# Mixed weight products between the halves of the neighbour products, y_hi ahead of relu on ScalarE, and the last neighbour products in other PSUM banks

## What is computed

```python
idx = top_k(-(sq[:, :, None] + sq[:, None, :] - 2 * einsum('bdn,bdm->bnm', xyz, xyz)), 8)   # xyz = ctx_4096, (4, 1601, 512)
for i in range(4):                                   # twice over: 8 layers in all
    shortcut = points                                # (4, 256, 512)
    p = where(points >= 0, points, 0.01 * points)
    g = neighbours of every point by idx             # (4, 256, 8, 512)
    c = einsum('oi,bin->bon', w[i], p)
    gn = einsum('oi,bikn->bokn', w[i], g)
    points = (c + gn.sum(axis=2)) / 9 + shortcut
```

## Time and profile before

| what | us |
|---|---|
| median of 3 runs | 337.64 (336.52 to 339.07) |
| the profiled execution | 334.24 |
| its span, first to last instruction | 332.5 |
| PE busy | 320.8 |
| DVE busy | 258.5 |
| ACT busy | 174.0 |
| POOL busy | 95.0 |

### The profile page before, as it was taken

The page is one execution under the profiler, slowest core; times in us unless marked ns, Lnnn a source line. Parts: engine busy times, 40 slices in busy tenths (PEclk is TensorE's granted clock), DMA queues, the critical chain, the costliest instruction groups (busy, mean ns, idle before and its releaser), DMA issues.

```text
span 332.5 us, 5114 instructions
## 1 busy us (share of the span) xinstructions
PE 320.8 (97%) x2024; PEld 290.9 (88%) x2024; DVE 258.5 (78%) x333; ACT 174.0 (52%) x255; POOL 95.0 (29%) x85
## 2 busy tenths in 40 slices
PE   4999999999999899999899999999999999999995
PEld 4999999999899788888788889888888888889884
DVE  3994799799699676888867796887869867796773
ACT  4584397485564726454836644626455264644510
POOL 2011111111133214333644441426335063441400
PEclk9999999999999999999999999999999999999999
DMA  7979859969700000000000000000000000000023
GB/s 236 353 209 264 223 146 239 279 150 251 188 0 1 2 0 2 0 0 2 1 2 0 1 3 0 0 2 0 2 0 0 2 0 2 0 0 2 38 92 126
DMA packets 8608, 23.41 MB, mean 70 GB/s; under 512 B 772, under 2 KB 2052, under 8 KB 8584
## 3 DMA queue, kind: packets, MB, share of 16 engines
q1 hardware_dynamic: 7288, 18.36, 16.3%
q0 software_dynamic: 1296, 4.72, 8.3%
HBM read 20.98 MB, written 2.10 MB: 69 GB/s over the span
## 4 chain that ended last, share of the span: by engine, by line
PE 41%; DVE 8%; ACT 2%; issue 1%; DVEq 0%
PE wide L423 24%; PE wide L412 6%; PE wide L401 5%; PE wide L399 5%; DVE y_rest L722 2%; DVE y_lo L726 2%; DVE r_mixed L662 2%; DVE state L734 2%; ACT y_hi L570 2%; ACT relu L562 1%; PE wide L385 0%; ACT r_high L565 0%; DVEq L709 0%; DVEq L725 0%
## 5 line engine op out<-in xcount | busy, mean ns | idle before, releaser
L279 POOL TENSOR_TENSOR r_low<-relu,r_high 128x512 fp32r<-128x512 f32 x64 | 84.8, 1339 | 140.4 <-ACT r_high L565 140.4
L423 PE MATMUL wide<-adj,y_hi 128*128 128x512 f32 (+1 forms) x260 | 102.3, 394 | 0.8 <-DVE state L734 0.8
L423 PE MATMUL wide<-adj,y_lo 128*128 128x512 f32 (+1 forms) x260 | 101.7, 393 | 0.0
L722 DVE TENSOR_TENSOR y_rest<-wide,y_hi 128x1024 f32<-128x1024 f32 x32 | 39.2, 1224 | 45.4 <-ACT y_hi L570 45.4
L562 ACT ACTIVATE relu<-state 128x512 f32<-128x512 f32 x64 | 40.2, 628 | 46.5 <-DVE state L734 33.7
L399 PE MATMUL wide<-w_high,r_high 128*128 128x256 f32 x256 | 62.2, 281 | 0.9 <-DVE y_rest L722 0.9
L401 PE MATMUL wide<-w_low,r_low 128*128 128x256 f32 x256 | 61.9, 280 | 0.0
L570 ACT CAST y_hi<-wide 128x1024 fp32r<-128x1024 f32 x32 | 32.3, 1008 | 54.8 <-PE wide L401 54.8
L423 PEld LDWEIGHTS wide<-adj,y_hi 128*128 128x128 f32 x260 | 48.9, 188 | 11.7 <-DVE state L734 1.2
L423 PEld LDWEIGHTS wide<-adj,y_lo 128*128 128x128 f32 x260 | 49.0, 188 | 10.5 <-issue 0.2
L399 PEld LDWEIGHTS wide<-w_high,r_high 128*128 128x128 f32 x256 | 48.3, 189 | 2.3 <-issue 1.1
(11 more groups left out here) (57 smaller groups left out, 290.6 us busy)
## 6 DMA issues: line engine op xcount, KB each, us to landing
raw<-in_ctx_dram SPq DMA_DIRECT2D x23, 512.0 KB, 5.4
g_low<-in_ctx_dram POOLq DMA_DIRECT2D x9, 512.0 KB, 6.2
state<-in_x_dram SPq DMA_DIRECT2D x4, 512.0 KB, 7.1
out_dram<-state SPq DMA_DIRECT2D x3, 512.0 KB, 2.8
w_raw<-in_fside_BxSxS_dram SPq DMA_DIRECT2D x1, 1024.0 KB, 11.2
rest_raw<-in_ctx_dram SPq DMA_DIRECT2D x4, 130.0 KB
raw<-in_ctx_dram SPq DMA_DIRECT2D x2, 256.0 KB, 3.3
out_dram<-state SPq DMA_DIRECT2D x1, 256.0 KB, 2.0
```

The costliest lines, as they stand in the source:

```text
L279: nc.gpsimd.tensor_tensor(r_low[:, n % 3, h, :], relu[:, h, :], r_high[:, n % 3, h, :].bitcast(fp32), ALU.subtract).then_inc(r_low_ready, 1)
L423: mm = nc.tensor.matmul(bank[to][:, cols], part[:, s % 2, q, h * P:(h + 1) * P], adj[:, b, q, cols], start=(q == 0 and part is y_hi), stop ...
L722: nc.vector.tensor_tensor(y_rest[:, :, :], wide[MAIN][:, :].rearrange("p (q o) -> p q o", q=NB), y_hi[:, s % 2, :, :].bitcast(fp32), ALU.s ...
```

## The change

Five edits:

- PE: the mixed products become a function of their own, `y_mixed`, and are issued between the two halves of the neighbour products of the step before (in step 0 right behind the main products).
- ACT: `y_high(s)` comes ahead of `relu_parts(s+1)`.
- DVE: `split_y` is cut in two. The order is y_rest of s, update of s-1 half 0, y_lo of s, (in step 1 distances and relu_mixed(2)), update of s-1 half 1, relu_mixed(s+1).
- The last neighbour products go to banks 6, 7 and 0.
- They wait for the updates of step 29 in place of those of step 30.

```diff
-        LAST_OUT = ((0, ALL, 4), (1, slice(0, N // 2), 5), (1, slice(N // 2, N), 0))
+        LAST_OUT = ((0, ALL, 6), (1, slice(0, N // 2), 7), (1, slice(N // 2, N), 0))
...
-            def y_step(s, w):
+            def y_main(s, w):
...
                 mm.then_inc(main_done, 1)
+
+            def y_mixed(s, w):
+
                 if s == 0:
                     pe.wait_ge(gram_ready, (B - 1) * NB + 3)
                 pe.wait_ge(r_mixed_ready, s + 1)
...
-                for n, (h, cols, to) in enumerate(pieces):
+                for n, (h, cols, to) in pieces:
...
-                y_step(s, l % BLOCKS)
+                y_main(s, l % BLOCKS)
+                if s == 0:
+                    y_mixed(s, l % BLOCKS)
...
-                    out_step(s - 1, STEPS[s - 1][1], out_pieces(s - 1))
+                    first_half, second_half = out_pieces(s - 1)
+                    out_step(s - 1, STEPS[s - 1][1], [first_half])
+                    y_mixed(s, l % BLOCKS)
+                    out_step(s - 1, STEPS[s - 1][1], [second_half])
...
-            pe.wait_ge(state_ready, CH * LAST_STEP)
-            out_step(LAST_STEP, STEPS[LAST_STEP][1], LAST_OUT)
+            pe.wait_ge(state_ready, CH * (LAST_STEP - 1))
+            out_step(LAST_STEP, STEPS[LAST_STEP][1], out_pieces(LAST_STEP))
...
             for s in range(B * LAYERS):
+                y_high(s)
                 if s + 1 >= B - 1 and s + 1 <= LAST_STEP:
                     relu_parts(s + 1)
-                y_high(s)
...
-            def split_y(s):
+            def y_remainder(s):
...
+            def y_low(s):
+
                 dve.wait_ge(mixed_done, s + 1)
...
-                split_y(s)
+                y_remainder(s)
+                if s > 0:
+                    update(s - 1, 0, ALL, 2 * out_at(s - 1), 0)
+                y_low(s)
                 if s == 1:
                     distances(B - 1)
                     relu_mixed(2)
                 if s > 0:
-                    update(s - 1, 0, ALL, 2 * out_at(s - 1), 0)
+                    update(s - 1, 1, ALL, 2 * out_at(s - 1) + 1, 1)
                 if B - 1 <= s + 1 <= LAST_STEP:
                     relu_mixed(s + 1)
-                if s > 0:
-                    update(s - 1, 1, ALL, 2 * out_at(s - 1) + 1, 1)
```

More of the change, by code:

```diff
@@ L146, in out_at @@
             return FIRST_WIDE if s < ENTER or s % 2 == 0 else SECOND_WIDE
+        assert out_at(LAST_STEP) == SECOND_WIDE
         def by_dma(b, k):
@@ L428, in out_pieces @@
             def out_pieces(s):
-                return LAST_OUT if s == LAST_STEP else tuple((h, ALL, 2 * out_at(s) + h) for h in range(CH))
+                return enumerate(LAST_OUT if s == LAST_STEP else ((h, ALL, 2 * out_at(s) + h) for h in range(CH)))
             for b in range(B):
```

## The result

The changed kernel takes 344.49 us (median of 4 runs, 344.02 to 345.14); the kernel before, 337.6 (4 runs). The ratio is 1.0213, with a 95% interval from 1.0176 to 1.0251: slower, by 6.9 us. The interval is clear of no change; whether the loss is more or less than 2% it does not tell.

What follows compares the result with a forecast made beforehand. PE was taken as the bound late (6.60 us of work a step), an ACT-DVE ring early (7.15). A new 7.13 us ring gave +9.8, the end -1.04, so +8.7 on 337.64: 346.3 us, range 341 to 353.

Steps and rivals of the forecast that it cites:

- y_hi ahead of relu: ACT's new order: the deciding term, making a loop of 7.13 us a step against 6.60 of PE's work.
- the ring: Loop over ACT, POOL and PE: main products, y_hi, relu and r_high twice, r_low twice, next main products; 7.13 us.
- 27c-183.8: Change of total time in us, where c is the length of one turn of the ring, forecast at 7.13.
- DVE's new order: DVE's reordered work: room enough, no cost after step 2; the early loop through ACT and DVE opens.
- r_low and r_mixed never meet: POOL and DVE: the new order keeps these two apart, so the pair of r_low stays at 2.55 us.
- Mixed products between the halves: PE: waits for r_mixed go, at most 0.07 us per late step, 0.55 per early; later y_lo, cover 2.3, costs nothing.
- Step 2: Mixed products now behind the wait for the state update: main(3) starts at 128.1 instead of 127.16, a lasting loss.
- Other banks: Last neighbour products: their wait for the update of the step before goes, -1.04 us (0 to -1.1).
- Rival 1: Faster, 332.0 us: r_low chain hidden, early ring opens, PE's 6.60 sets each step; needs c below 6.81; chance 0.05.
- Rival 2: About even, 337.2 us: POOL's r_low ready some 0.34 earlier than recorded, ring 6.79; chance 0.06.
- Rival 3: Slower still: PE learns of POOL's end 0.5 late, 354 us, or r_low pairs stretch, 375; 0.06 together with Rival 4.
- Rival 4: PE's hole of 0.5 in each step could cost its granted clock; not priced; chance 0.06 together with Rival 3.

Runs made afterwards that it cites:

- e1: The changed kernel with ACT's old order put back (relu_parts(s+1), then y_high(s)); 332.27 us, ratio 0.9889 to the kernel before.
- e2: The kernel before with ACT's order alone changed, y_high(s) ahead of relu_parts(s+1); 343.4 us, ratio 1.023.
- e5: The changed kernel, but POOL starts its first r_low only when both halves of r_high are there; 378.52 us in a single run.
- e6: The changed kernel with relu_parts(s+1) of half 0 ahead of y_high(s) and of half 1 behind it; 330.32 us, ratio 0.9843.
- e7: e6 with PE's mixed products back ahead of both halves of the neighbour products, DVE's new order kept; 348.39 us, ratio 1.0369.
- e3: The kernel before with only the last neighbour products' new banks and their wait on step 29's updates; 335.3 us against 336.13, ratio 0.9975.

## Why the prediction was right

The forecast was 346.3 (341 to 353) and slower; measured 344.5. Point by point:

- *y_hi ahead of relu.* Shown, from both sides: e1 and e2 switch the ring off and on by that edit alone, e5 and e6 lengthen and shorten it. Its terms: main products 1.78 in the forecast; last product to y_hi 0.31, measured 0.32; y_hi to the end of r_low 4.84, measured 4.84; hop from POOL to PE 0.20, for which 258.53-0.12-258.26 gives 0.15 in the rows above. The step is 7.07, where I had 7.13.
- *The size.* The forecast's 27c-183.8 gives +7.1 with c = 7.07, and measured are 6.9 by the medians and 7.3 by the second phase. The 1.6 us between +8.7 and +7.1 are 27 times 0.06, and 0.05 of each 0.06 is the hop, taken too long. It was the one term without a row, and the nearest row was another engine's.
- *DVE's new order.* It costs nothing here: DVE is busy for 29.85 of 35.40 us in the early steps. The forecast read its room from the kernel before, where r_mixed seldom met an r_low in those steps; with ACT's old order the same DVE order fills DVE in the early steps (e1).
- *r_low and r_mixed never meet.* Right: the page has r_mixed at a mean of 1.22 for 1.47 before, and r_low at 1.30 for 1.34. What the forecast did not value is what that avoids: e7 shows 0.83 in each step where they meet on the ring.
- *Mixed products between the halves.* No wait for r_mixed is left, and y_lo has a cover of 260.30-257.45 = 2.85 us, where I had 2.3. But the forecast put the worth of this part at no more than 0.07 in a late step and 0.55 in an early one. With DVE's new order and an open ring it is worth more: e7, without it, is 18 us slower than e6. So DVE's new order without the new place of the mixed products is harmful. The new place without DVE's new order was not run.
- *Step 2.* main(3) was to start at 128.1. It starts at 130.51, and the second phase began 2.4 later, so 128.1 on the old scale. The 1.2 us wait on L428 is the hole in front of the neighbour products in step 2; the view names no releaser ("issue"), but DVE's update ends at 125.07, right ahead of it:

```profile
124.39 0.68 DVE L747 SCALAR_TENSOR_TENSOR state<-wide,state 128x512 f32<-128x512 f32 x1
...
125.17 0.47 PE L428 MATMUL wide<-adj,y_hi 128*128 128x512 f32 x1 [1.18 <-issue]
```

- *Other banks.* -1.04 expected, and e3 shows 12.27 to 11.2.
- *Rival 1* (faster, 332.0, that is -5.6) had about the right price for an open ring, and in part by luck. e1 gives 332.3, -3.9 by the medians and -5.0 from the mixed products of step 0 to the end. It has PE's own work at 6.57 a step where the forecast had read 6.60 from a single one, and it loses some 1.2 in the early steps, where DVE is full, which the forecast did not see. The rival's condition did not hold here, since nothing was missing from the recorded chain. *Rival 2* needed r_low 0.34 faster than recorded. The page of the Trainium skill that I set beside it, "GPSIMD Engine Reference", section "Elementwise — side-by-side cycle accounting" (2.6 cycles an element, by which I estimated 1.11 us), is low here: r_low alone takes 1.28 to 1.30, and e5 shows that PE waits for those ends. *Rival 3* needed a hop of 0.5 or a stretched pair: the hop is 0.15 to 0.17, and from step 3 on no r_low takes more than 1.32. *Rival 4*: PE's pitch is that of before, and e2, with the same holes, has the granted clock recorded at 1.00, the level of 2.4 GHz.

Left open: what makes the first phase end anywhere between 109.1 and 113.3 us with the same code. In the two latest, of e5 and e7, 3.4 us of it ran at a granted clock of 0.50; for the others no cause is shown.

## What to carry to other kernels

Before an operation is moved ahead of another on an in-order engine, follow what the second one feeds, round to the first one's own releaser: if that closes a loop, its length is a floor for every step, however idle its engines are. Here ACT was busy half the time and POOL a quarter, and they set the pace by latency alone. A late link of such a chain can be split: with half of relu ahead of y_hi and half behind it, y_hi came early enough and the loop stayed under PE's work (e6). Against the old order with all of relu ahead (e1) that saved 1.1 us in steps 3 to 8, by one trace each, and nothing in the late steps.

Look also for an occurrence of the new order in the old trace. The whole chain but its last hop stood there in one step, with its gaps, and it was right to 0.01 us.

## What the runs showed of the hardware beyond what was expected

- Where r_mixed on DVE (both inputs in SBUF) and an r_low on POOL overlap, they do not slow one another down evenly: the one that started first keeps its own time, and the other one waits for it. In the rows of e1 r_low ends at 146.30 and r_mixed at 147.37, and the next r_low at 148.53; in the step of e7 it is 257.18 and 258.26. In all 103 overlaps of the eleven traces the later one ends 1.08 to 1.10 us after the earlier one if it is r_mixed (89 of them), and 1.14 to 1.16 if it is r_low (14). That is its time alone (1.22 or 1.30) less 0.14. So the stretch can be worked out from the starts: in e7 r_mixed starts 0.32 after an r_low of 1.29, and 1.29-0.32-0.14 = 0.83; the pair of 3.62 in the earlier trace rows has 1.22-0.14 = 1.08 added.
- PE takes up work 0.15 to 0.17 us after the end of the POOL operation that it waited for, less than the 0.22 seen behind DVE, although POOL's spans are called rough.
